# Graph attention on one core: id rows compared a group ahead, edge attributes transposed at the head of the next step

## The reference

```python
h = relu(layernorm(x)) @ W.T                # 3125 x 128, 8 heads of 16
e = a_src[src] + a_dst[dst]; e = where(e >= 0, e, 0.2 * e)
p = exp(e - segment_max(e, dst)[dst])
out = segment_sum(p / segment_sum(p, dst)[dst] * h[src], dst) + bias
```

```python
score = einsum('ehd,ehd->eh', q[dst], k[src]) / 4 + edge_attr @ We + be
out = segment_sum(softmax_by_dst(score) * v[src], dst) @ Wo + bo
```

## Time and profile before

| | us |
|---|---|
| median of 3 runs | 1561.53 (1558.28 to 1563.58) |
| the profiled execution | 1565.84 |
| its span in the trace | 1564.1 |
| the 23 groups of gathers from 135.61 to 700.44 us, first layer | 564.83 |
| granted TensorE clock, mean | 0.658 |

### The profile page before, as it was taken

One profiled execution on the slowest core, in us unless ns is written; L12 is line 12 of the kernel. 1 busy time (PEld: TensorE's weight loads), 2 busy tenths in 40 slices (PEclk: granted clock), 3 DMA queues, 4 the chain that ended last, 5 costly groups with the idle time before them and its releaser, 6 DMA issues. The chain is left out here.

```text
span 1564.1 us, 21265 instructions
## 1 busy us (share of the span) xinstructions
PE 1022.3 (65%) x4985; PEld 859.9 (55%) x4985; DVE 934.4 (60%) x3002; ACT 638.2 (41%) x1699; POOL 880.9 (56%) x926
## 2 busy tenths in 40 slices
PE   5546666656757766667475567666767767676775
PEld 4335554545545555555365456656656666565664
DVE  6446656556566655657823465656566565656577
ACT  5524343343434434422463344434344444444414
POOL 5756666666666666662056566665666555666400
PEclk9655556565565555655776687787776676778665
DMA  6322222222222222122133232322232222332201
GB/s 138 80 55 54 60 51 60 52 59 61 54 57 54 61 60 55 45 60 80 51 109 95 79 85 85 88 84 78 83 87 85 81 85 81 85 88 84 68 1 42
DMA packets 56924, 110.37 MB, mean 71 GB/s; under 512 B 17421, under 2 KB 31393, under 8 KB 56677
## 3 DMA queue, kind: packets, MB, share of 16 engines
q0 software_dynamic: 36288, 91.12, 22.5%
q1 hardware_dynamic: 19203, 17.39, 3.9%
q10 hardware_dynamic: 1313, 0.50, 0.1%
HBM read 100.60 MB, written 8.81 MB: 70 GB/s over the span
## 5 line engine op out<-in xcount | busy, mean ns | idle before, releaser
L528 POOL DMA_INDIRECT G<-table,idx_all x880 | 854.6, 971 | 524.2 <-issue 272.7
L857 PE MATMUL bank<-PV,S 128*125 128x144 f32 x1760 | 456.3, 420 | 134.2 <-DVE acc L1431 79.7
L857 PEld LDWEIGHTS bank<-PV,S 128*125 128x125 f32 x1760 | 379.8, 291 | 157.6 <-issue 82.5
L1431 DVE TENSOR_TENSOR acc<-acc,bank 125x144 f32 x880 | 260.3, 296 | 291.0 <-PE bank L857 155.4
L632 ACT ACTIVATE S<-iota_n,lid 128x125 f32<-128x125 f32 x880 | 275.8, 387 | 0.4 <-issue 0.4
L841 PE MATMUL bank<-qe,ST 125*128 x880 | 163.6, 355 | 93.4 <-DVE prod L1230 67.8
L841 PEld LDWEIGHTS bank<-qe,ST 125*128 125x128 f32 x880 | 152.6, 264 | 106.1 <-issue 106.1
L642 ACT ACTIVATE ST<-bank 125x512 f32<-125x512 f32 x110 | 63.7, 595 | 284.5 <-PE bank L828 153.2
L1408 DVE TENSOR_TENSOR PV<-G,PV 128x512 f32<-128x512 f32 x220 | 151.1, 688 | 22.4 <-issue 20.8
L636 ACT ACTIVATE S<-S,ones 128x500 f32<-128x500 f32 x220 | 156.6, 712 | 8.9 <-ACT S L632 1.9
L828 PE MATMUL bank<-ident,S 128*125 128x128 f32 x440 | 101.1, 369 | 30.7 <-issue 24.2
(11 more groups left out here) (219 smaller groups left out, 1125.7 us busy)
## 6 DMA issues: line engine op xcount, KB each, us to landing
G<-table,idx_all POOLq DMA_INDIRECT x880
prod<-in_edge_attr_dram SPq DMA_DIRECT2D x26, 224.0 KB
table<-G SPq DMA_DIRECT2D x12, 224.0 KB
bias_rows<-qe SPq DMA_DIRECT2D x1, 1664.0 KB
table<-h0b SPq DMA_DIRECT2D x8, 178.5 KB
out_dram<-G SPq DMA_DIRECT2D x8, 168.0 KB
prod<-in_edge_attr_dram SPq DMA_DIRECT2D x26, 30.0 KB
xs<-in_x_dram SPq DMA_DIRECT2D x1, 504.0 KB
```

Of the source, the lines that this page charges most:

```text
L528: pool.indirect_dma_start(G[:, u, v, 0:w], None, table, bass.IndirectOffsetOnAxis(ap=idx_all[:, g * GV + v:g * GV + v + 1], axis=0)).then_ ...
L857: pe.matmul(sums_bank(p)[0:BN, at:at + H * SLOT], S[:, ur, v, :], PV[:, v, :, :].rearrange("p h k -> p (h k)"), start=True, stop=True).the ...
L1431: ve.tensor_tensor(a, a, o, ALU.add).then_inc(s.sem["acc_added"], 1)
```

## The change

The buffer of the one-hot matrix becomes two, chosen by the group's parity, in the whole of `ST_`. Step g now spreads and compares the ids of group g + 1; `expand` in the step finds them ready, and its quarters 0 and 1 move up, behind the first and second batch of sums. The four compares leave the first half of VectorE's step for its second half. The attribute transposes leave the end of step g for the head of step g + 1, behind the transposed scores, and ScalarE's copy of them stands at the head of its step, ahead of `esT`. `pace` is unchanged. Step 0 spreads and compares its own group first.

```diff
--- before.py
+++ after.py
@@ -123,7 +123,7 @@
         S = sb("S", [P, UNROLL, GV, BN])
         ST_ = sb("ST", [P, GV, P])
         ST = ST_[0:BN, :, :]
-        ST_b = ST_[0:BN, :, :].rearrange("p v e -> p (v e)").bitcast(BF16)[:, 0:GV * P].rearrange("p (v e) -> p v e", v=GV)
+        ST_b = ST_[0:BN, :, :].rearrange("p v e -> p (v e)").bitcast(BF16).rearrange("p (d v e) -> p d v e", d=2, v=GV)
         PV = sb("PV", [P, GV, H, SLOT])
         prod = sb("prod", [P, UNROLL, QV * F])
         attr_in = prod
@@ -646,6 +646,10 @@
                     q = g - 1
                     k = 2 - n
                     following = (g + 1) % UNROLL
+                    if n == 0 and mid and q < AG:
+                        wait(act, a_T, q + 1)
+                        wait(act, a_mm, q)
+                        act.activation(attrT[:, :], tp[0][:, :], ACT.Copy).then_inc(a_Te, 1)
                     if mid and n == 0:
                         wait(act, s["scoreT"], q + 1)
                         wait(act, s["dd_ready"], 2 * q)
@@ -671,11 +675,6 @@
                         wait(act, a_mm, q + 1)
                         act.activation(eb_nat[:, bass.ds(q * (ATTR_C * H), ATTR_C * H)], sm[:, 256:256 + ATTR_C * H],
                                        ACT.Copy).then_inc(a_out, 1)
-                    if new:
-                        if n == 0 and has_attr(g, new):
-                            wait(act, a_T, g + 1)
-                            wait(act, a_mm, g)
-                            act.activation(attrT[:, :], tp[0][:, :], ACT.Copy).then_inc(a_Te, 1)
                     if mid:
                         wait(act, s["al_mm"], q + 1)
                         wait(act, s["rescaled"], q)
@@ -816,8 +815,8 @@
                     if j == 0:
                         pe.wait_ge(s_lid[u], 16 * (i + 1))
                     wait(pe, s["st_ready"], 4 * g + j - 1)
-                    if j == 0:
-                        wait(pe, a_Te, attr_done(g - 1))
+                    if j == 0 and g > 1:
+                        wait(pe, a_Te, attr_done(g - 2))
                     pe.matmul(tp[j % 2][0:BN, :], ones_b[32 * u:32 * u + 1, :], lid_ring[32 * u:32 * u + 1, j * QV * P:(j + 1) * QV * P],
                               start=True, stop=True).then_inc(s.sem["t_done"], 1)
 
@@ -840,7 +839,7 @@
                         if n:
                             last = pe.matmul(ex[j % 2][:, k * F:k * F + F], ST[:, v, :], nodes[:, bass.ds(off, F)], start=True, stop=True)
                             continue
-                        last = pe.matmul(ex[v // 8][:, v % 8 * width:(v % 8 + 1) * width], ST_b[:, v, :],
+                        last = pe.matmul(ex[v // 8][:, v % 8 * width:(v % 8 + 1) * width], ST_b[:, g % 2, v, :],
                                          nodes[:, bass.ds(off, width)], start=True, stop=True)
                     last.then_inc(s.sem["expanded"], 1)
 
@@ -860,9 +859,10 @@
 
                 def step(g, u, i, new, mid, old):
                     q = g - 1
-                    if new and n == 0:
-                        spread_ids(g, u, i, 0)
-                        spread_ids(g, u, i, 1)
+                    ahead, ua, ia = quarters(g + 1), (g + 1) % UNROLL, (g + 1) // UNROLL
+                    if n == 0 and g == 0:
+                        for j in range(new):
+                            spread_ids(g, u, i, j)
                     if mid:
 
                         wait(pe, s["scores_ready"], q + 1)
@@ -873,14 +873,21 @@
                             wait(pe, s["esT_ready"], q)
                             pe.transpose(sT[:, P:2 * P], es[:, 1, :, :].rearrange("p v h -> p (v h)"), ident[:, :])
                         pe.transpose(sT[:, 0:P], sc[:, :, :].rearrange("p v h -> p (v h)"), ident[:, :]).then_inc(s.sem["scoreT"], 1)
+                    if n == 0 and mid and q < AG:
+                        pe.wait_ge(s_attr[q % UNROLL], 48 * (q // UNROLL + 1))
+                        wait(pe, a_Te, q)
+                        wait(pe, s["st_ready"], 4 * g + 3)
+                        for k in range(QV):
+                            last = pe.transpose(tp[0][:, k * P:k * P + P], attr_in[:, q % UNROLL, k * P:k * P + P], ident[:, :])
+                        last.then_inc(a_T, 1)
                     if new:
                         pe.load(regs, offs[1 if n else 2][:, bass.ds(g * GV, GV)])
                     if new and n:
                         one_hot_T(g, u, 0)
                     if 3 * old > 0:
                         sums(g, u, 0)
-                    for j in range(2, 0 if n else new):
-                        spread_ids(g, u, i, j)
+                    if new and n == 0:
+                        expand(g, 0)
                     if mid:
                         wait(pe, s["rh_ready"], q + 1)
                         wait(pe, s["x_done"], q)
@@ -892,6 +899,8 @@
                                   start=True, stop=True).then_inc(s.sem["hop1"], 1)
                     if 3 * old > 2:
                         sums(g, u, 1)
+                    if new > 1 and n == 0:
+                        expand(g, 1)
                     if new and n:
                         one_hot_T(g, u, 1)
                     if mid:
@@ -904,9 +913,6 @@
                             last = pe.matmul(sm[:, 64 + GV * k:64 + GV * k + GV], HselT[:, :, :].rearrange("p v h -> p (v h)"),
                                              d[:, k, k:k + GV], start=True, stop=True)
                         last.then_inc(s.sem["hop2"], 1)
-                    if new and n == 0:
-                        expand(g, 0)
-                        expand(g, 1)
                     if new > 2 and n:
                         one_hot_T(g, u, 2)
                     if n == 0 and mid and q < AG:
@@ -918,6 +924,8 @@
                         last.then_inc(a_mm, 1)
                     if 3 * old > 4:
                         sums(g, u, 2)
+                    for j in range(0 if n else min(ahead, 2)):
+                        spread_ids(g + 1, ua, ia, j)
                     if new and n:
                         expand(g, 0)
                         expand(g, 1)
@@ -929,14 +937,10 @@
                         expand(g, 2)
                     if new > 3:
                         expand(g, 3)
+                    for j in range(2, 0 if n else ahead):
+                        spread_ids(g + 1, ua, ia, j)
                     if 3 * old > 8:
                         sums(g, u, 4)
-                    if n == 0 and has_attr(g, new):
-                        pe.wait_ge(s_attr[u], 48 * (i + 1))
-                        wait(pe, a_Te, g)
-                        for k in range(QV):
-                            last = pe.transpose(tp[0][:, k * P:k * P + P], attr_in[:, u, k * P:k * P + P], ident[:, :])
-                        last.then_inc(a_T, 1)
                     if mid:
 
                         wait(pe, s["p_ready"], q + 1)
@@ -1212,12 +1216,12 @@
                             off.extend(ve.snap(x, min_val=0, max_val=(BLOCKS - 1) * H * SLOT) for x in half)
 
 
-                    def node_rows(j):
-                        if j >= new or n == 1:
-                            return
-                        wait(ve, s["t_done"], 4 * g + j + 1)
-                        wait(ve, s["expanded"], 4 * (g - 1) + j + 1)
-                        ve.tensor_scalar(ST_b[:, QV * j:QV * j + QV, :],
+                    def node_rows(to, j):
+                        if j >= quarters(to) or n == 1:
+                            return
+                        wait(ve, s["t_done"], 4 * to + j + 1)
+                        wait(ve, s["expanded"], 4 * (to - 2) + j + 1)
+                        ve.tensor_scalar(ST_b[:, to % 2, QV * j:QV * j + QV, :],
                                          tp[j % 2][0:BN, :].rearrange("p (v e) -> p v e", v=QV), node, None,
                                          op0=ALU.is_equal).then_inc(s.sem["st_ready"], 1)
 
@@ -1433,22 +1437,21 @@
 
                     if n == 0 and g == GROUPS - 1:
                         bias_parts()
-                    node_rows(0)
+                    if g == 0:
+                        for j in range(4):
+                            node_rows(g, j)
                     load_offsets(0)
                     weigh(0)
-                    node_rows(1)
                     load_offsets(1)
                     loop_max()
                     weigh(1)
                     edge_scans()
                     rescale()
                     edge_maxima()
-                    node_rows(2)
                     add(0)
                     visit_scans()
                     add(1)
                     carry()
-                    node_rows(3)
                     add(2)
                     weigh(2)
                     outer_maxima()
@@ -1462,9 +1465,11 @@
                     differences()
                     weigh(3)
                     add(7)
+                    node_rows(g + 1, 0)
                     shrink()
                     qk_product(0)
```

(3 more changed lines are left out.)

## The result

The changed kernel takes 1579.57 us (median of 4 runs, 1572.95 to 1582.38); the kernel before, beside it, 1559.9 us (1557.85 to 1563.58). The ratio is 1.010, with a 95% interval of 1.0063 to 1.0136: slower by 1.0%, where 2.2% was forecast. The profiled execution took 1578.07 us (before: 1565.84).

What follows compares the result with a forecast made beforehand. GpSimd with its pauses was taken as the bound: 20.0 + 3 x 2.0 = 26.0 us a group against 24.56, so +1.4 in 25 groups, 35 us on the median 1561.5, gives 1596 us; range 1538 to 1638.

Steps and rivals of the forecast that it cites:

- The bound: First layer: GpSimd's gathers, 20.0 us a group, plus two pauses of 2.0 us made by late-seen TensorE signals.
- The fifth batch: TensorE's sums, behind spreads 2 and 3: start some 4.5 us behind the opening add instead of 2.0.
- The scores: VectorE, with compares 2 and 3 ahead: 3 to 4 us later, eating the slack but for 0.6 us.
- The pause ahead of visit 4: GpSimd: a third pause because the fifth batch ends late; 0.7 to 2.0 us, 2.0 taken; chance 0.38.
- the forecast's own sign of being wrong: Two pauses or fewer, groups of 24.4 us or less, although scores come later; or a fifth batch as early as before.
- 20.0 + 3 x 2.0 = 26.0 us: First-layer group: gathers plus three pauses of 2.0 us, against 24.56 before: +1.4 us in each of 25 groups.
- the 0.56 us between 24.0 and 24.56: Rest of the mean group before, taken as extra pauses in less regular groups and not added again.
- Fewer pauses: Rival: pause at visit 4 removes that at visit 8; up to 1.7 us a group gained, middle 0.9, 1539 us; chance 0.28.
- Out of step: Rival: `hop1` about 8 us into the row waits for a pause at visit 12; 3 us a group, 1636 us; chance 0.20.
- The attribute work: Transposes and ScalarE's copy moved to the step's head, ahead of `esT`: costs 0 to 1.66 us a group.
- The compares: VectorE: four a group moved, none added; idle time going with their old places at most 0.8 us a group.
- the prediction's sentence: A TensorE signal that comes late in an unbroken row of gathers is seen when the gathers stop.

Runs made afterwards that it cites:

- ca_both: Changed kernel with attribute work back at the end of the step and spreads 2 and 3 behind the fifth batch; late sitting: 1572.49 us, ratio 1.005 to before.
- a_attr: Changed kernel with attribute transposes back at the end of the step and ScalarE's copy in its old place; late sitting: 1580.28 us, ratio 1.011 to before.
- before_again: The kernel before, unchanged, run again for its trace in the second sitting, a late one: 1566.57 us.
- b_nopace: The kernel before without the waits of `pace` in the first layer; prompt sitting: 1327.55 us, ratio 0.999 to before.
- a_nopace: The changed kernel without the waits of `pace` in the first layer; late sitting: 1697.37 us, ratio 1.086 to before.
- after: The changed kernel's first trace, late sitting: profiled execution 1578.07 us, median 1579.57 us, ratio 1.010 to before.
- after_fast: The changed kernel, unchanged, in the sixth sitting, a prompt one: 1318.26 us, ratio 0.997 to before.
- b_gap: The kernel before with a one-element GpSimd memset behind every first-layer gather from the second group on; prompt sitting: 1323.1 us, ratio 0.998 to before.

## Why the prediction was half right

**What held.** The bound, and what moves it: GpSimd with its pauses, fed by late signals of TensorE. The fifth batch: 4.5 us behind the add forecast, 4.4 measured. The scores: 3 to 4 us later forecast, 4.2 measured. The pause ahead of visit 4: in all 23 groups, 1.73 us a group (0.7 to 2.0 given, 2.0 taken). That the spreads ahead of the batch are its cause: mostly, by ca_both against a_attr. The direction, and the range of 1538 to 1638 us; but the direction held by luck in part. In 17 of 23 groups of the changed kernel the forecast's own sign of being wrong stands: two pauses, 24.24 us, although the scores come later. The loss is in the other six, which no case had.

**What failed** is the sum "20.0 + 3 x 2.0 = 26.0 us". It treats a pause as a piece with a fixed price that one adds to the others. It isn't: a pause lasts until a certain signal is through, and behind a full pause the signals are prompt for a while, so a new pause pays a part of the next one. In a_attr, the edit for which the third pause does stand there, the three together are 4.5 us a group, where two were 3.6 before (the earlier trace rows have 2.0 and 2.0 in one group). In the changed kernel the pauses are 5.0 to 5.2 us, before 4.1 to 4.2: +0.9 to +1.1 instead of +2.0. The gathers' own time fell by 0.3 to 0.4 us a group beside it (11 and 12 of the 368 gathers take over 1 us instead of 32 and 34), a term that the sum didn't have. Net +0.6 to +0.7, where +1.4 was forecast. That the forecast was +1.4 and not +2.0 rests on a wrong reading, too: the sum took the 0.56 us between 24.0 and 24.56 as extra pauses of irregular groups. The table has 15.53 us of gathers where 16 x 0.94 are 15.04, so most of it is gathers that take longer than 0.94.

**The rivals were taken as exclusive, and came together.** "Fewer pauses" said that the pause ahead of visit 4 takes away the one ahead of visit 8: right, in all 23 groups. "Out of step" said that `hop1` over 6 us behind a restart waits for a pause ahead of visit 12: right, at 7.7 us, in 21 of 23. Its price of 3 us was wrong, since with that pause made, the one ahead of visit 0 shrank from 2.29 to 0.62 in the ordinary groups. These ordinary groups are even shorter than before, by 0.1 to 0.3 us where "fewer pauses" had 0.9. What none of the cases had is the edge between them: where `hop1` ends about 7.5 us behind the restart, its signal mostly comes through early, the pause is missed or cut short, `hop2` is seen late, and that group costs 2 to 6 us. (That `hop1`'s distance is the cause is read from where the long groups lie; no run moved `hop1` alone in a late sitting.) I had met late signals in a row without a pause in the earlier trace rows and didn't ask what follows when a pause is made one group and missed in the next.

**The attribute work** had the bounds 0 and 1.66 us a group. Its place moves the pauses from visits 0, 4, 8 to 4 and 12, and the time by nothing that can be told (25.21 against 25.16 and 25.27 us). **The compares**: the idle time ahead of them went to 0.0 from 27.8 us, or 1.3 us a group, in before_again (18.1 in the trace that I had, from which I gave 0.8 at most); nobody gained from it, since the time went to the wait for `hop1`.

**What wasn't known** is that the mechanism isn't there in every sitting. The forecast of +2.2% was made for the kind that the profile showed; in the other kind the change is worth -0.3%.

## What to carry to other kernels

Don't price a stall by its count times its length: ask what ends it and how long what comes next is prompt, and add up a group again from there. Where a pause is made in most groups and missed or cut short in some, look for those; their mean hides six groups of 23 with all of the loss. And take out a wait only after asking what else goes through in the time that it makes: here the waits of `pace` are worth 7% where signals are late and nothing where they are not.

## What the runs showed of the hardware that I had not expected

**The same kernel at 1325 and at 1565 us.** Medians of the kernel before in the seven sittings: 1330.11, 1566.57, 1325.47, 1327.29, 1325.39, 1324.19, 1564.82 us. The fifth and the seventh were on the same chip. It isn't in the first layer alone: the second, from its first gather to group 27's, takes 678.0 us in the trace of before and 555.1 in that of b_nopace, whose edit doesn't touch it. The gathers have the same spacing of 1.25 us in both kinds, so the spacing alone isn't what holds signals back, as the prediction's sentence could be read. In the 23 groups of before_again, 49 silences of TensorE's signals of over 1 us end in a pause; the first signal behind them comes 1.40 us behind the last gather's end (median) and the last landing signal of that gather 1.59 us. There they come through at about the same time; those of a_nopace that come through in the middle of a row don't fit this. What puts a sitting into one kind or the other no run here shows.

The Trainium skill (SBUF — State Buffer, Who interferes with whom) has DMA and the compute engines never contend. The prompt sittings agree: the reader of `hop1` waits 2.6 us in 20 groups. The late ones don't (69.2 us in 21), if it is contention that holds the signals back; what does, no run here shows.

**Gathers get longer beside one operation of VectorE.** In b_nopace 86 of the 368 gathers take over 1 us instead of 0.94, and 82 of these lie beside a `weigh` (L1408, `PV` from `G` and `PV`, both in SBUF). One of them, with an ordinary one ahead:

```profile
410.50 0.94 POOL L528 DMA_INDIRECT G<-table,idx_all  x1 [0.30 <-issue]
...
411.63 0.67 DVE L1408 TENSOR_TENSOR PV<-G,PV 128x512 f32<-128x512 f32 x1
...
411.75 1.38 POOL L528 DMA_INDIRECT G<-table,idx_all  x1 [0.31 <-issue]
```

The gather takes 0.44 us more, and the `weigh` keeps its 0.67. How much more depends on how much of the `weigh` is left. In before_again, after, b_nopace and after_fast 229 gathers start inside a `weigh`; 225 of them end 0.82 us behind its end, within 0.02, or take the usual 0.94 where under 0.12 us of it was left. (The other four start together with it and take 0.94.) In after_fast it is 73 gathers, 65 of them beside a `weigh`, and the gathers' own time is 16.05 us a group instead of 16.30: with the two 0.3% apart this fits the small gain of the prompt sittings, but which moved instruction does it wasn't tried. The Trainium skill (SBUF — State Buffer, Who interferes with whom) states an exclusive lock for such a pair, a VectorE operation with two inputs in SBUF and a GpSimd operation that reads SBUF; the traces agree for the gather that starts behind the `weigh`. So an engine can wait for another one without any semaphore.

**0.30 us between two gathers is room.** A memset of 0.09 us in it costs nothing (b_gap).
